# Attention of a fused graph block: three fp16 hi/lo products on 64x64 tiles in place of block-diagonal float32 products

## The chip, the cores and the metric

One core of one Trainium2 chip runs the whole program. The metric is the device time of one execution in microseconds (us), here the median of three runs. The profile is one more execution, taken by the hardware profiler; its times are given from the start of its span.

## The reference

`x` is (128, 64, 512): 128 batches of 64 nodes with 512 features. `adj` is a symmetric 0/1 matrix of 64x64 with ones on its diagonal. Cut to what matters:

```python
# layer 0
x = layernorm(x + (einsum('bnf,nm->bmf', x, adj * adj) + bias))
# layer 1
z_l = einsum('bnd,ed->bne', x, W_lang);  z_g = einsum('bnd,ed->bne', x, W_grav)
v   = einsum('bnd,ed->bne', x, W_V)
zn  = z_l / max(norm(z_l), EPS)
A_l = max(zn @ zn.T, 0) * not_eye                 # 64x64 per batch
d2  = max(|z_g|^2 + |z_g|^2.T - 2 z_g @ z_g.T, 0)
A_g = exp(-d2 / (2 sigma^2)) * not_eye
K_l, K_g = (A * adj) / max(rowsum(A * adj), EPS)  # for A_l and A_g
K   = sigmoid(gate) * K_l + (1 - sigmoid(gate)) * K_g
x   = layernorm(x + (K @ v) @ W_O.T)
```

## The kernel before, in words

The 128 batches are worked on in 16 groups of 8. A group is four pairs of batches: a pair `p` fills the 128 partitions, batch 2p in rows 0 to 63, batch 2p+1 in rows 64 to 127. Each engine has its own instruction stream, written out by hand; semaphores join them. `iteration(g, ...)` is what an engine does for group g, together with the front of group g+1 (`nxt`: layer 0, its normalisation, the split and the transposes) and the end of group g-1 (`before`: attention, residual, final normalisation). Fourteen of the sixteen iterations have both neighbours.

The weights are folded before the loop. Both similarities are quadratic forms, h W'W h', so their matrices are built once (`l_hi`, `l_lo`: the lower triangle with half a diagonal, so that a later step adds the transpose), and W_V and W_O are folded into one matrix (`m_hi`, `m_lo`). Each fp32 factor is split in an fp16 high part and the fp16 rest, and a product is three: hi·hi, hi·lo, lo·hi. fp32 products remain in a few places; a fp32 product shows as two matmuls of the trace.

TensorE does, per iteration (function, line):

- `mix` (L339), four: layer 0 of the next group, fp32, two before and two after `project(g, 0)`.
- `project(g, j)` (L359), j = 0 to 7: 12, 9, 6, 3, 12, 9, 6, 3 products of 512 columns, into three PSUM banks in turn.
- `kernel_t(before)` (L416): transposes the attention matrices `ks_sb` of the group before, behind project 1.
- `attend(before, p)` (L429), four, behind project 2: `kt` is a block-diagonal 128x128 fp32 matrix (two batches, zeros between), `u` is h·M in fp32.
- `values(g, p)` (L375), four of 12 products; `gram` (L389), 96 products of 64 columns, behind values 0; `symmetrise` (L400) behind values 1; `spread` (L409) behind values 2.

ScalarE copies `p_hi` (L557) from PSUM, VectorE subtracts it from PSUM to give `p_lo` (L736); a project's bank is free only then, and gram needs all eight. Likewise `h_hi` on ScalarE (L543) and `h_lo` on VectorE or GpSimd (L731, L1065). ScalarE also copies `u` (L562) and `kt` (L580), applies the final normalisation to `o` (L593), and issues the eight DMA transposes per group (L550), spread between its instructions, which bring h_hi and h_lo to `ht_hi`, `ht_lo`, with features on the partitions. VectorE does the residual o = attention + h (L811), statistics (L713, L815), the normalisation h (L726), and the chain from `t_diag` through `diag`, `nsq`, `vec` to `v_diag` and from `ps_v` to the weights `ks_sb`. GpSimd does the inverse standard deviations (L1026, L1028), two h_lo, `t_diag` (L1048) and inverse norms (L1054, L1055), in this order. SyncE issues the x loads and the stores of a whole group.

The order in which the VectorE stream takes p_low, residual and norm_rows, and the order of p_high and h_high on ScalarE, are fixed by the text of their `iteration`.

Of the kernel before, what the change touches and what calls it, by code (L numbers as in the profile page):

```python
# [28 lines left out]
P = 128  # L29
# [25 lines left out]
def resnorm_graph_kernel(nc, x, adj, bias, w_lang, w_grav, w_v, w_o, gate, log_sigma, out):  # L55
# [18 lines left out]
    with ctx:  # L74
# [16 lines left out]
        ht_lo = [sb(f"ht_lo{i}", [P, DC, ROWS], F16) for i in range(2)]  # L91
        p_hi = sb("p_hi", [P, DC, GB, 2, N], F16)
        p_lo = sb("p_lo", [P, DC, GB, 2, N], F16)
        u = sb("u", [P, PAIRS, D])
# [10 lines left out]
        kt = sb("kt", [P, PAIRS, P])  # L105
# [22 lines left out]
        w_raw["v"] = u  # L128
# [37 lines left out]
        wv_scale = sb("wv_scale", [P, 1])  # L166
# [51 lines left out]
        u_ready = sem("u_ready")  # L218
# [18 lines left out]
        kt_ready = sem("kt_ready")  # L237
# [18 lines left out]
        def over_batches(square_, lo=0, hi=P):  # L256

            return square_[lo:hi, :].unsqueeze(1).to_broadcast([hi - lo, GB, N])

# [6 lines left out]
        def _(sp):  # L266
# [27 lines left out]
            reload(Group(0, 0))  # L294
            with sp.Fori(0, G // 2 - 2) as i:
                reload(Group(i, 1))
                store(Group(i, 0))
                reload(Group(i + 1, 0))
                store(Group(i, 1))
            last = G // 2 - 2  # L300
            reload(Group(last, 1))
            for g in (Group(last, 0), Group(last, 1), Group(last + 1, 0)):
                store(g)

            end = Group(last + 1, 1)
# [19 lines left out]
        def _(pe):  # L325
# [16 lines left out]
            def project(g, j, first):  # L342
# [6 lines left out]
                if j < 3:  # L349
                    if first:  # L350
                        pe.wait_ge(m_copied, j + 1)
                    else:
                        pe.wait_ge(u_ready, g.prev().count(4, j + 2))
                else:
                    pe.wait_ge(plo_ready, g.count(8, j - 2))
                passes = [(k, a, b) for k in range(c, DC)
                          for a, b in ((l_hi, ht_hi), (l_hi, ht_lo), (l_lo, ht_hi))]
                for n, (k, a, b) in enumerate(passes):
                    mm = pe.matmul(proj[j % 3][:, :], a[s][:, blk(k, c), :], b[g.parity][:, k, :],  # L359
                                   start=(n == 0), stop=(n == len(passes) - 1))  # L360
                mm.then_inc(proj_done, 1)

            def values(g, p, first=False):
# [4 lines left out]
                else:  # L368
                    pe.wait_ge(u_ready, g.count(4, 1))
                passes = [(k, a, b) for k in range(DC)  # L370
                          for a, b in ((ht_hi, m_hi), (ht_hi, m_lo), (ht_lo, m_hi))]
                for n, (k, a, b) in enumerate(passes):
                    if first and p == 0 and n % 3 == 0:
                        pe.wait_ge(wt_lo, 2 + k + 1)
                    mm = pe.matmul(proj[j % 3][:, :], a[g.parity][:, k, p * P:(p + 1) * P], b[:, k, :],  # L375
# [3 lines left out]
            def gram(g, first):  # L379
# [7 lines left out]
                for b in range(GB):  # L387
                    for n, (c, a, t) in enumerate(passes):
                        mm = pe.matmul(ps_t[:, b * N:(b + 1) * N],  # L389
                                       a[:, c, b, :, :].rearrange("p s n -> p (s n)"),  # L390
                                       t[g.parity][:, c, b * N:(b + 1) * N],
# [12 lines left out]
            def spread(g, first):  # L404

                pe.wait_ge(v_ready, g.count(1, 1))
                if not first:
                    pe.wait_ge(kt_ready, g.prev().count(2, 2))
# [22 lines left out]
            def last_residual(g, p):  # L431

                if p < 2:
                    pe.wait_ge(sum_ready, g.prev().count(4, (4, 2)[p]))
                elif p == 2:
                    pe.wait_ge(sum_ready, g.prev().count(4, 3))
                pe.matmul(last_ku_bank[p][:, :], ident[:, :], h[g.parity][:, p, :], start=True, stop=False)

            def back(g):
                kernel_t(g)  # L440
                pe.wait_ge(kt_ready, g.count(2, 2))
                pe.wait_ge(u_ready, g.count(4, 4))
                for p in range(PAIRS):
                    pe.matmul(last_ku_bank[p][:, :], kt[:, p, :], u[:, p, :], start=(p == 3), stop=True).then_inc(ku_done, 1)

            def iteration(g, has_prev, has_next):
# [21 lines left out]
                if has_prev:  # L468
                    for p in range(PAIRS):
# [3 lines left out]
                project(g, 7, first)  # L473
# [8 lines left out]
                else:  # L482
                    last_residual(g, 0)
                    last_residual(g, 1)
# [7 lines left out]
                    last_residual(g, 2)  # L492
# [47 lines left out]
        def _(act):  # L540
            def h_high(g, p):
                act.wait_ge(h_ready, g.count(4, p + 1))
                act.activation(h_hi[:, p, :], h[g.parity][:, p, :], ACT.Copy).then_inc(hhi_ready, 1)  # L543

            def transposes(g, first, last):


                for n in range(first, last):
                    p, part, part_t = n // 2, (h_hi, h_lo)[n % 2], (ht_hi, ht_lo)[n % 2]
                    act.dma_start_transpose(part_t[g.parity][:, :, p * P:(p + 1) * P],  # L550
                                            part[:, p, :]).then_inc(ht_loaded[g.parity], 16)
# [8 lines left out]
            def u_copy(g, p):  # L560
                act.wait_ge(proj_done, g.count(12, 9 + p))
                act.activation(u[:, p, :], proj[(8 + p) % 3][:, :], ACT.Copy).then_inc(u_ready, 1)  # L562
# [13 lines left out]
            def kt_copy(g):  # L576
                act.wait_ge(kt_done, g.count(1, 1))
                for q in range(2):
                    half = slice(q * N, (q + 1) * N)
# [541 lines left out]
```

## Time and profile before

| | |
|---|---|
| median of 3 runs | 627.4 us (626.99 to 628.38) |
| span of the profiled execution, first to last instruction | 625.0 us |
| mean granted TensorE clock | 0.998 of full |
| TensorE busy | 614.2 us (98%) |
| VectorE busy | 444.2 us (71%) |
| ScalarE busy | 242.7 us (39%) |
| GpSimd busy | 155.5 us (25%) |
| attention products (L429), share of the chain that ended last | 8% |
| DMA transposes | 128, 13.4% of the 16 DMA engines' span |

The profiled execution has no time of its own beyond the span: the device time of a run also holds what lies before the first and behind the last instruction, and the median of the runs is 2.4 us above the span. Busy time of TensorE is not the same as columns streamed, since matmuls are pipelined and each is shown until its result is out; the chain in order of time shows what each piece really occupies.

### The profile page before, as it was taken

How to read it: one execution, taken by the hardware profiler on the slowest of the kernel's cores; microseconds unless marked ns; L12 is line 12 of the kernel's file. 1: busy time of each engine (PE TensorE's matmuls, PEld its weight loads, DVE VectorE, ACT ScalarE, POOL GpSimd, SP SyncE). 2: the span in 40 equal slices, each digit the busy share in tenths (PEclk: the TensorE clock that was granted, in tenths of full speed). 3: DMA queues.
4: the chain of work that ended last, by engine and by line, in shares of the span. 5: the costliest groups of instructions: out<-in, count | busy, mean ns of one | idle time of the engine just before them, and what ended most of it. 6: DMA issues, size and time to landing. Idle time of an engine off the chain costs nothing.

```text
span 625.0 us, 11961 instructions
## 1 busy us (share of the span) xinstructions
PE 614.2 (98%) x4468; PEld 315.0 (50%) x4468; DVE 444.2 (71%) x940; ACT 242.7 (39%) x413; POOL 155.5 (25%) x159
## 2 busy tenths in 40 slices
PE   9999999999999999999999999999999999999994
PEld 6543545454454545454454545445454545545452
DVE  1759486877868586876868687786858788686564
ACT  2345224333443424434432433344342443443333
POOL 1002205032231403123230503223140312323021
PEclk9999999999999999999999999999999999999999
DMA  8722203434123342423223342312334242302103
GB/s 269 244 44 87 51 1 68 136 53 125 52 62 116 64 134 60 141 42 87 90 50 134 67 134 55 120 51 58 119 67 134 59 143 42 92 17 51 69 2 135
DMA packets 89392, 55.05 MB, mean 88 GB/s; under 512 B 70816, under 2 KB 70816, under 8 KB 89376
## 3 DMA queue, kind: packets, MB, share of 16 engines
q1 hardware_dynamic: 19744, 38.05, 17.9%
q10 hardware_dynamic: 69632, 16.79, 13.4%
q8 instruction: 10, 0.16, 0.1%
q14 instruction: 6, 0.05, 0.0%
HBM read 21.27 MB, written 16.78 MB: 61 GB/s over the span
## 4 chain that ended last, share of the span: by engine, by line
PE 96%; DVE 2%; ACT 1%; POOL 0%; issue 0%; POOLq 0%; ACTq 0%; DVEq 0%
PE proj L359 31%; PE proj L375 27%; PE front L339 9%; PE ps_t L389 7%; PE front L429 4%; PE ps_k L429 4%; PE ps_t L400 3%; PE ps_v L409 2%; PE proj L499 2%; PE proj L529 2%; PE ps_v L416 2%; PE ps_t L499 1%; PE ps_k L329 1%; DVE p_lo L736 1%; PE ps_t L529 1%; DVE y L709 0%
## 5 line engine op out<-in xcount | busy, mean ns | idle before, releaser
L557 ACT ACTIVATE p_hi<-proj 128x512 f16<-128x512 f32 x128 | 75.9, 593 | 118.2 <-PE proj L359 117.7
L736 DVE TENSOR_TENSOR p_lo<-proj,p_hi 128x512 f16<-128x512 f32 x128 | 86.0, 688 | 20.9 <-ACT p_hi L557 17.9
L375 PE MATMUL proj<-m_hi,ht_hi 128*128 128x512 f16 x256 | 97.2, 380 | 0.7 <-DVE p_lo L736 0.7
L375 PE MATMUL proj<-m_hi,ht_lo 128*128 128x512 f16 x256 | 97.0, 379 | 0.0
L375 PE MATMUL proj<-m_lo,ht_hi 128*128 128x512 f16 x256 | 97.0, 379 | 0.0
L1026 POOL TENSOR_TENSOR ve<-mv,eps_ln 128x4 f32<-128x4 f32 x31 | 6.6, 212 | 307.7 <-DVE mv L718 211.5
L562 ACT ACTIVATE u<-proj 128x512 f32<-128x512 f32 x64 | 37.9, 592 | 82.7 <-PE proj L375 82.5
L543 ACT ACTIVATE h_hi<-h 128x512 f16<-128x512 f32 x64 | 36.5, 619 | 69.0 <-DVE h L726 69.0
L1065 POOL TENSOR_TENSOR h_lo<-h,h_hi 128x512 f16<-128x512 f32 x30 | 41.5, 1403 | 84.4 <-ACT h_hi L543 84.4
L359 PE MATMUL proj<-ht_hi,l_grav_hi 128*128 128x512 f16 x160 | 60.6, 379 | 0.6 <-DVE p_lo L736 0.6
L359 PE MATMUL proj<-ht_hi,l_lang_hi 128*128 128x512 f16 x160 | 60.8, 380 | 0.0
L359 PE MATMUL proj<-ht_lo,l_grav_hi 128*128 128x512 f16 x160 | 60.6, 379 | 0.0
L359 PE MATMUL proj<-ht_hi,l_grav_lo 128*128 128x512 f16 x160 | 60.6, 379 | 0.0
L359 PE MATMUL proj<-ht_lo,l_lang_hi 128*128 128x512 f16 x160 | 60.6, 379 | 0.0
L359 PE MATMUL proj<-ht_hi,l_lang_lo 128*128 128x512 f16 x160 | 60.6, 379 | 0.0
L339 PE MATMUL front<-x_in,wmix 128*128 128x512 f32 x128 | 60.2, 593 | 0.0
L593 ACT ACTIVATE o<-o,nmr,rstd 128x512 f32<-128x512 f32 x60 | 46.9, 807 | 9.7 <-issue 9.3
L709 DVE TENSOR_TENSOR y<-front,bias_b 128x512 f32<-128x512 f32 x64 | 42.5, 686 | 11.3 <-PE front L339 10.8
L389 PE MATMUL ps_t<-ht_hi,p_lo 128*128 128x64 f16 x512 | 46.5, 193 | 0.0
L389 PE MATMUL ps_t<-ht_lo,p_hi 128*128 128x64 f16 x512 | 46.5, 193 | 0.0
L389 PE MATMUL ps_t<-ht_hi,p_hi 128*128 128x64 f16 x512 | 46.5, 193 | 0.0
L389 PEld LDWEIGHTS ps_t<-ht_hi,p_hi 128*128 128x128 f16 x512 | 45.1, 98 | 2.3 <-issue 0.5
(166 smaller groups left out, 1051.8 us busy)
## 6 DMA issues: line engine op xcount, KB each, us to landing
x_in<-in_x SPq DMA_DIRECT2D x16, 1024.0 KB, 7.1
out<-o SPq DMA_DIRECT2D x15, 1024.0 KB, 5.0
w_raw_lang<-in_L_gnn_W_lang SPq DMA_DIRECT2D x4, 256.0 KB, 3.1
o<-in_L_gnn_W_O SPq DMA_DIRECT2D x1, 1024.0 KB, 10.2
w_raw_grav<-in_L_gnn_W_grav SPq DMA_DIRECT2D x4, 256.0 KB, 10.1
u<-in_L_gnn_W_V SPq DMA_DIRECT2D x1, 1024.0 KB, 12.0
ht_hi<-h_hi ACTq DMA_TRANSPOSE x64, 2.4
ht_lo<-h_lo ACTq DMA_TRANSPOSE x64, 2.5
```

The lines of the kernel that those rows point to most:

```text
L339: pe.matmul(front[p % 2][:, :], wmix[:, :], x_in[g.parity][:, p, :], start=True, stop=True).then_inc(l0_done, 1)
L359: mm = pe.matmul(proj[j % 3][:, :], a[s][:, blk(k, c), :], b[g.parity][:, k, :], start=(n == 0), stop=(n == len(passes) - 1))
L375: mm = pe.matmul(proj[j % 3][:, :], a[g.parity][:, k, p * P:(p + 1) * P], b[:, k, :], start=(n == 0), stop=(n == len(passes) - 1))
L389: mm = pe.matmul(ps_t[:, b * N:(b + 1) * N], a[:, c, b, :, :].rearrange("p s n -> p (s n)"), t[g.parity][:, c, b * N:(b + 1) * N], start=( ...
L429: pe.matmul(ku_bank[p][:, :], kt[:, p, :], u[:, p, :], start=True, stop=True).then_inc(ku_done, 1)
L543: act.activation(h_hi[:, p, :], h[g.parity][:, p, :], ACT.Copy).then_inc(hhi_ready, 1)
L557: act.activation(p_hi[:, j % 4, :, j // 4, :], by_batch(proj[j % 3]), ACT.Copy).then_inc(phi_ready, 1)
L562: act.activation(u[:, p, :], proj[(8 + p) % 3][:, :], ACT.Copy).then_inc(u_ready, 1)
L593: act.activation(o[:, p, :], o[:, p, :], ACT.Identity, scale=rstd2[:, p:p + 1], bias=nmr2[:, p:p + 1]).then_inc(out_ready, 1)
L709: dve.tensor_tensor(y[:, p, :], front[p % 2][:, :], bias_b[:, :], ALU.add).then_inc(y_ready, 1)
L736: dve.tensor_tensor(p_lo[:, j % 4, :, j // 4, :], by_batch(proj[j % 3]), p_hi[:, j % 4, :, j // 4, :], ALU.subtract).then_inc(plo_ready, 1)
L1065: pool.tensor_tensor(h_lo[:, p, :], h[g.next().parity][:, p, :], h_hi[:, p, :], ALU.subtract).then_inc(hlo_ready_pool, 1)
```

## The change

`u` and `kt` are kept as fp16 pairs (`u_hi`, `u_lo`; `kt_hi`, `kt_lo`, no zero blocks). The attention of a group is two halves `a` = 0, 1; each has three passes (hi·hi, lo·hi, hi·lo as above) of four products with 64 rows, 64 output partitions and 512 columns, on the four quadrants of the array. Half 0 follows project 3, half 1 follows project 4, and the waits stand ahead of the last product of that project. For this the batches of a pair in `ht`, and so in `u`, are paired anew: the transposes take 64 rows and 1024 columns each (two pairs of batches), and are issued by SyncE (only those of the first group still by ScalarE), with `h_hi`, `h_lo` and `ht` laid out by feature chunk. SyncE's loop is written out. VectorE gets `u_low` and `kt_low`; the residual applies a scale; norm_rows is cut in two, and h_low moves behind the p_low. The last group no longer adds h through TensorE (`last_residual`), but by residual. Cut to its core:

```diff
-        h_hi = sb("h_hi", [P, PAIRS, D], F16)
-        h_lo = sb("h_lo", [P, PAIRS, D], F16)
-        ht_hi = [sb(f"ht_hi{i}", [P, DC, ROWS], F16) for i in range(2)]
+        h_hi = sb("h_hi", [P, 2, DC, 2, P], F16)
+        h_lo = sb("h_lo", [P, 2, DC, 2, P], F16)
+        ht_hi = [sb(f"ht_hi{i}", [P, PAIRS, DC, P], F16) for i in range(2)]
...
+        def transposes(queue, g, a):
+            for split, split_t in ((h_hi, ht_hi), (h_lo, ht_lo)):
+                for j in range(2):
+                    queue.dma_start_transpose(
+                        split_t[g.parity][:, 2 * a + j, :, :].rearrange("p c (q n) -> p (c q) n", q=2),
+                        split[j * N:(j + 1) * N, a, :, :, :].rearrange("p c q e -> p (c q e)"),
+                    ).then_inc(ht_loaded[g.parity], 16)
...
+            def turn(g):
+                sp.wait_ge(hlo_ready, g.count(2, 4))
+                transposes(sp, g, 0)
+                sp.wait_ge(hlo_ready_pool, g.count(2, 0))
+                transposes(sp, g, 1)
+            groups = [Group(n // 2, n % 2) for n in range(G)]
+            reload(groups[0])
+            for n, g in enumerate(groups):
+                if n + 3 < G:
+                    reload(groups[n + 1])
+                if n + 1 < G:
+                    turn(groups[n + 1])
+                if n > 0:
+                    store(groups[n - 1])
...
-            def attend(g, p, mixed):
-                if mixed and p in (1, 2):
-                    pe.wait_ge(y_ready, mixed.count(4, p + 2))
-                if p == 0:
-                    pe.wait_ge(kt_ready, g.count(2, 2))
-                    pe.wait_ge(u_ready, g.count(4, 4))
-                elif p == 3:
-                    pe.wait_ge(sum_ready, g.count(4, 1))
-                pe.matmul(ku_bank[p][:, :], kt[:, p, :], u[:, p, :], start=True, stop=True).then_inc(ku_done, 1)
+            def attend_waits(g, a, nxt):
+                if a == 0:
+                    pe.wait_ge(ktlo_ready, g.count(1, 1))
+                    pe.wait_ge(ulo_ready, g.count(4, 4))
+                else:
+                    pe.wait_ge(sum_ready, g.count(4, 1))
+                if nxt:
+                    pe.wait_ge(y_ready, nxt.count(4, 3 + a))
+            def attend(g, a, banks):
+                passes = ((kt_hi, u_hi), (kt_hi, u_lo), (kt_lo, u_hi))
+                for n, (kt, u) in enumerate(passes):
+                    for q in range(2):
+                        half = slice(q * N, (q + 1) * N)
+                        for side in range(2):
+                            mm = pe.matmul(banks[2 * a + q][side * N:(side + 1) * N, :], kt[half, 2 * a + side, :],
+                                           u[half, 2 * a + side, :], start=(n == 0), stop=(n == len(passes) - 1))
+                mm.then_inc(ku_done, 1)
...
                 project(g, 2, first)
-                if has_prev:
-                    for p in range(PAIRS):
-                        attend(before, p, nxt)
-                for j in range(3, 7):
+                for a in range(2):
+                    project(g, 3 + a, first, (before, a, nxt) if has_prev else None)
+                    if has_prev:
+                        attend(before, a, ku_bank)
+                for j in range(5, 8):
                     project(g, j, first)
...
+            def u_low(g, p):
+                dve.wait_ge(uhi_ready, g.count(4, p + 1))
+                dve.tensor_tensor(u_lo[:, p, :], proj[(8 + p) % 3][:, :], u_hi[:, p, :],
+                                  ALU.subtract).then_inc(ulo_ready, 1)
+            def kt_low(g):
+                dve.wait_ge(kthi_ready, g.count(1, 1))
+                dve.tensor_tensor(kt_lo[:, :, :], ps_v[:, 0:PAIRS * N].rearrange("p (a n) -> p a n", a=PAIRS),
+                                  kt_hi[:, :, :], ALU.subtract).then_inc(ktlo_ready, 1)
```

VectorE, the middle of an iteration, from the second p_low to the statistics of the output. Before (o is the residual, h the normalised rows, y and stats layer 0 and its statistics):

```order
L736 TENSOR_TENSOR p_lo<-proj,p_hi 128x8x64
L718 BN_AGGR mv<-stats 128x2 x4
...
L811 TENSOR_TENSOR o<-ps_k,h 128x512
...
L736 TENSOR_TENSOR p_lo<-proj,p_hi 128x8x64
L722 ISA
L726 TENSOR_SCALAR h<-y,mv,rstd 128x512 x4
L731 TENSOR_TENSOR h_lo<-h,h_hi 128x512
L735 REGISTER_ALU
L736 TENSOR_TENSOR p_lo<-proj,p_hi 128x8x64
L731 TENSOR_TENSOR h_lo<-h,h_hi 128x512
```

The same place in the changed stream, from p_low(4) on:

```order
L738 TENSOR_TENSOR p_lo<-proj,p_hi 128x8x64
L823 SCALAR_TENSOR_TENSOR o<-front,ku_scale,h 128x512
L823 SCALAR_TENSOR_TENSOR o<-ps_k,ku_scale,h 128x512
...
L728 TENSOR_SCALAR h<-y,mv,rstd 128x512
...
L738 TENSOR_TENSOR p_lo<-proj,p_hi 128x8x64
L727 REGISTER_ALU
L728 TENSOR_SCALAR h<-y,mv,rstd 128x512 x2
...
L738 TENSOR_TENSOR p_lo<-proj,p_hi 128x8x64
L733 TENSOR_TENSOR h_lo<-h,h_hi 128x4x128 x2
L828 BN_STATS stats<-o 128x6 x4
```

The four h stood behind the third p_lo, ahead of five more; now two stand between the fifth and the sixth, two between the sixth and the seventh, and the h_lo behind the eighth, ahead of the statistics.

ScalarE, the same stretch, before:

```order
L557 ACTIVATE p_hi<-proj 128x8x64
L542 ISA
L543 ACTIVATE h_hi<-h 128x512
...
L543 ACTIVATE h_hi<-h 128x512
L556 REGISTER_ALU
L557 ACTIVATE p_hi<-proj 128x8x64
L542 REGISTER_ALU
L543 ACTIVATE h_hi<-h 128x512
```

And changed, from p_high(4) to p_high(7):

```order
L578 ACTIVATE p_hi<-proj 128x8x64
L571 ISA
L572 ACTIVATE h_hi<-h 128x4x128
L571 REGISTER_ALU
L572 ACTIVATE h_hi<-h 128x4x128
L577 REGISTER_ALU
L578 ACTIVATE p_hi<-proj 128x8x64
L571 REGISTER_ALU
L572 ACTIVATE h_hi<-h 128x4x128
L571 REGISTER_ALU
L572 ACTIVATE h_hi<-h 128x4x128
L577 REGISTER_ALU
```

Three h_hi stood between p_hi 2 and 3 and one between 3 and 4; now two stand between p_hi 4 and 5, two between 5 and 6.

## Rows read from the trace of the kernel before

**Rows 1.** The page: busy time, and the chain that ended last by engine

```profile
PE 614.2 (98%) x4468; PEld 315.0 (50%) x4468; DVE 444.2 (71%) x940; ACT 242.7 (39%) x413; POOL 155.5 (25%) x159
...
PE 96%; DVE 2%; ACT 1%; POOL 0%; issue 0%; POOLq 0%; ACTq 0%; DVEq 0%
```

**Rows 2.** The chain in order of time, 312 to 364 us: start us, us, what

```profile
314.71 2.80 PE ps_t L389 x96
...
321.18 2.69 PE proj L375 x12
...
323.88 0.86 PE ps_v L409 x2
...
327.32 1.72 PE front L339 x4
...
337.31 0.86 PE ps_k L429 x2
...
340.74 7.12 PE proj L359 x33
...
363.07 1.29 PE front L339 x3
```

**Rows 3.** Timeline of VectorE, 327 to 364 us: start, us, engine, line, work [idle before]

```profile
336.10 0.69 DVE L736 TENSOR_TENSOR p_lo<-proj,p_hi 128x512 f16<-128x512 f32 x1
...
347.90 1.31 DVE L736 TENSOR_TENSOR p_lo<-proj,p_hi 128x512 f16<-128x512 f32 x2 [0.63 <-ACT p_hi L557]
349.13 2.46 DVE L815 BATCH_NORM_STATS2 stats<-o 128x6 f32<-128x512 f32 x4
...
351.70 0.37 DVE L821 BATCH_NORM_AGGREGATE mv<-stats 128x2 f32<-128x6 f32 x4
...
355.40 0.69 DVE L742 TENSOR_REDUCE diag<-t_diag 128x8 f32<-128x512 f32 x1 [1.77 <-POOL t_diag L1048]
...
358.13 0.69 DVE L750 TENSOR_TENSOR v_diag<-eye,vec 128x512 f32<-128x512 f32 x1 [1.65 <-POOL vec L1054]
...
360.51 0.69 DVE L762 SCALAR_TENSOR_TENSOR s_sb<-s_sb,ps_v 64x512 f32<-64x512 f32 x1 [1.09 <-PE ps_v L409]
```

**Rows 4.** Timeline of TensorE, first products of symmetrise

```profile
355.77 0.27 PE L400 MATMUL ps_t<-eye_l,t_sb 128*64 128x64 f32 x1
355.78 0.27 PE L400 MATMUL ps_t<-eye_g,t_sb 128*64 128x64 f32 x1
```

**Rows 5.** Groups by line and form: count, busy us, mean ns, idle before

```profile
L375 PE MATMUL proj<-m_hi,ht_hi 128*128 128x512 f16 x256 | 97.2, 380 | 0.7 <-DVE p_lo L736 0.7
...
L736 DVE TENSOR_TENSOR p_lo<-proj,p_hi 128x512 f16<-128x512 f32 x128 | 86.0, 688 | 20.9 <-ACT p_hi L557 17.9
L557 ACT ACTIVATE p_hi<-proj 128x512 f16<-128x512 f32 x128 | 75.9, 593 | 118.2 <-PE proj L359 117.7
...
L726 DVE TENSOR_SCALAR h<-y,mv,rstd 128x512 f32<-128x512 f32 x64 | 30.5, 540 | 2.1 <-POOL rstd L1028 2.1
...
L580 ACT ACTIVATE kt<-ps_v 64x256 f32<-64x256 f32 x32 | 12.1, 378 | 2.0 <-PE ps_v L416 1.2
```

**Rows 6.** Timeline of GpSimd, 352 to 356 us

```profile
352.15 0.20 POOL L1026 TENSOR_TENSOR ve<-mv,eps_ln 128x4 f32<-128x4 f32 x1 [5.09 <-DVE mv L821]
352.43 1.01 POOL L1028 TENSOR_TENSOR rstd<-ve,minus_half 128x4 f32<-128x4 f32 x1
354.10 1.27 POOL L1048 TENSOR_TENSOR t_diag<-t_sb,eye 128x512 f32<-128x512 f32 x1 [0.67 <-ACT t_sb L570]
```

**Rows 7.** Timeline of ScalarE, the h_hi of three pairs

```profile
342.55 1.67 ACT L543 ACTIVATE h_hi<-h 128x512 f16<-128x512 f32 x3 [4.61 <-DVE h L726]
```

**Rows 8.** Timeline of ScalarE's queue, and the page's DMA issues

```profile
347.90 1.20 ACTq L550 DMA_TRANSPOSE ht_hi<-h_hi  x1
349.14 1.29 ACTq L550 DMA_TRANSPOSE ht_lo<-h_lo  x1
...
ht_hi<-h_hi ACTq DMA_TRANSPOSE x64, 2.4
```

More of the change, by code:

```diff
@@ L104, in resnorm_graph_kernel @@
         ks_sb = sb("ks_sb", [P, ROWS])
-        kt = sb("kt", [P, PAIRS, P])
+        kt_hi = sb("kt_hi", [P, PAIRS, N], F16)
+        kt_lo = sb("kt_lo", [P, PAIRS, N], F16)
         stats1 = sb("stats1", [P, PAIRS, 6])
@@ L293, in _ @@
             load(Group(0, 1))
[L294 to L305, printed above, removed]
+            def turn(g):
[12 more added lines that the diff above has]
+                    store(groups[n - 1])
+            end = groups[-1]
             for p in range(PAIRS):
@@ L340, in mix, with project @@
                           start=True, stop=True).then_inc(l0_done, 1)
-            def project(g, j, first):
+            def project(g, j, first, attended=None):
                 c, s = j % 4, ("lang", "grav")[j // 4]
@@ L542, in h_high @@
                 act.wait_ge(h_ready, g.count(4, p + 1))
[L543 to L551, printed above, removed]
+                act.activation(by_chunk(h_hi, p), chunks(h[g.parity], p), ACT.Copy).then_inc(hhi_ready, 1)
             def p_high(g, j, first):
@@ L617, in iteration @@
                 if has_prev:
-                    kt_copy(before)
+                    kt_high(before)
                 p_high(g, 2, first)
+                p_high(g, 3, first)
+                p_high(g, 4, first)
                 if has_next:
@@ L805, in scale_rows, with residual @@
                 dve.tensor_tensor(by_batch(ks_sb), by_batch(a_sb), over_columns(cfac), ALU.mult).then_inc(ks_ready, 1)
-            def residual(g, p, first):
-                dve.wait_ge(ku_done, g.count(4, p + 1))
-                if p == 0 and not first:
+            def residual(g, p, banks):
+                dve.wait_ge(ku_done, g.count(2, p // 2 + 1))
+                if p == 0:
                     dve.wait_ge(o_moved, g.prev().count(16, 32))
-                dve.tensor_tensor(o[:, p, :], ku_bank[p][:, :], h[g.parity][:, p, :], ALU.add).then_inc(sum_ready, 1)
+                dve.scalar_tensor_tensor(out=o[:, p, :], in0=banks[p][:, :], scalar=ku_scale[:, 0:1],
+                                         in1=h[g.parity][:, p, :], op0=ALU.mult, op1=ALU.add).then_inc(sum_ready, 1)
             def out_stats(g, p):
@@ L930, in iteration @@
                 p_low(g, 5)
+                if has_next:
+                    norm_rows(nxt, 1, before)
                 if first:
@@ L934, in iteration @@
                 p_low(g, 7)
+                if has_next:
+                    h_low(nxt, 0)
+                    h_low(nxt, 1)
                 if has_prev:
@@ L944, in iteration @@
                 diagonals(g)
+                u_low(g, 1 if has_next else 0)
                 diagonal_matrices(g)
                 sums(g)
+                if not has_next:
+                    u_low(g, 1)
                 distances(g)
+                u_low(g, 2)
             dve.memset(ones[:, :], 1.0).then_inc(dve_const, 1)
```

177 lines of the change are left out of this document (80 added, 97 removed).

## The prediction

> **What bounds the kernel now.** I read the page first. TensorE is busy for 98% of the span and the chain that ended last runs over it for 96% [rows 1]: as it stands, a microsecond of TensorE removed from a group would be a microsecond gained, if nothing else comes last in its place. Next the chain in order of time. The reader is to see that one group is 35.75 us (the mixes of two groups start at 327.32 and 363.07), that the pieces follow each other without a gap, and that the attention products fill it from 337.31 to 340.74, so 3.43 us [rows 2]. Then VectorE and GpSimd, since the change puts work there: they are off the chain, but not by much. The chain's stamps lie 0.16 us behind the starts of the other views (it follows ends). So gram starts at 314.71 + 35.75 - 0.16 = 350.30, and the last p_lo ends at 347.90 + 1.31 = 349.21: 1.09 us ahead. The spread starts at 323.88 + 35.75 - 0.16 = 359.47, and v_diag ends at 358.82: 0.65 us ahead [rows 2, 3]. These two distances decide the case.
>
> **What TensorE saves.** A full 512-column fp16 product costs 7.12/33 = 0.216 us [rows 2]. The new attention is two halves of twelve 64x64 products each. Whether four such tiles run together no row shows. What rows show is two column tiles running together: an eye_l and an eye_g product start 10 ns apart and run 0.27 us beside each other [rows 4]. The two column tiles there have their own moving data. I take four together, so three rounds, 0.65 us a half. A change of tile shape costs about 0.10 us on each side: the twelve products behind the two-column tiles take 2.69 [rows 2] in place of 12 x 0.216 = 2.59, and I put the same on the way in. A half is then 0.85, both are 1.70, and TensorE saves 3.43 - 1.70 = 1.73 us a group. Ends: two together, 2 x (1.30 + 0.20) = 3.0; one at a time, 24 x 0.216 + 0.4 = 5.6.
>
> The Trainium skill (TensorE: Matmul & The Clock Gate, Part 3, on packing) gives 3.07 times, not 4, for four row tiles; by that, as an estimate, a half is 1.04 and the result some 4 us later. No row here shows row tiles at all.
>
> **What is added elsewhere.** VectorE gets four u_lo (psum in, fp16 out, the form of p_lo, 0.69 each [rows 5]; four instructions of that length in a row take 2.46, so they start 0.60 apart [rows 3]) and kt_lo, half as wide; between ScalarE's kt of the same width, 0.378, and p_lo's 0.69 [rows 5] I take 0.42. The residual keeps its size as a scalar_tensor_tensor. ScalarE has one kt_hi for two kt and loses the issue of transposes. What matters is where the moved steps stand: norm_rows of the next group now comes behind p_low(4) and all four residuals, its second half behind p_low(5); h_high(0), (1) stand ahead of p_high(5), h_high(2), (3) ahead of p_high(6); h_low and the four statistics follow p_low(7). Four waits of TensorE result. I price each from its release, with 0.03 us from one engine's end to the next one's start (t_diag ends at 355.37, diag starts at 355.40 [rows 3, 6]) and 0.16 us from a product's issue slot to its end (0.379 - 0.216 [rows 5]).
>
> *Wait A, ahead of the last product of project 3, for kt_lo.* Now VectorE goes from s_sb at 360.51 (1.04 us behind the spread's start) to the end of the second p_lo at 336.10 + 0.69, one period on: 12.03 us [rows 3]. Two u_lo add 1.2 and kt_lo 0.33 behind p_lo; they fill some 0.4 of small waits of that stretch. So kt_lo is there 1.04 + 13.2 = 14.2 after the spread's start. TensorE's own work to that product is 337.31 - 323.88 = 13.43, plus two products: 13.86 [rows 2]. Stall 0.35.
>
> *Wait B, values(0) for p_lo 5.* From the end of project 4's slots: 0.16 to its end, p_hi 0.60, p_lo, residual, residual at 0.60 each, norm 0.54, two h_hi at 0.53 (three take 1.67 [rows 7]), p_hi 0.60, p_lo 0.69 [rows 5], hand-overs: 5.6 us. TensorE has attend(1) 0.85 and projects 5 to 7, 18 products, 3.89: 4.74. Stall 0.87.
>
> *Wait C, gram for p_lo 7.* From p_lo 5's end: norm, started 0.09 before, ends at 0.45, h_hi at 0.48 and 1.01, p_hi 6 at 1.53, p_hi 7 at 2.02 (a tenth inside the one before, as with h_hi), p_lo 6 at 2.16, p_lo 7 from 2.77 to 3.46. TensorE has values(0), 2.59. Stall 0.87.
>
> *Wait D, spread for v_diag.* From p_lo 7's end: two h_lo end their slots at 1.11, statistics and aggregates take 2.94 (349.13 to 352.07), GpSimd's ve and rstd are done 1.37 later, so at 5.42. t_sb is long there, but t_diag is behind rstd in GpSimd's queue: it ends at 6.72. From t_diag's end (355.37) to v_diag's (358.82) is 3.45 [rows 3, 6]: 10.2. TensorE needs 323.88 - 314.71 = 9.17 from gram to spread [rows 2]. Stall 1.0.
>
> The stalls sum to 3.09, TensorE saves 1.73: **a group grows by 1.36 to 37.1 us**. Fourteen such iterations give 19.0. The first one has no attention to save and C-like waits: 0.7, an estimate. In the last, three products with ident go (2.6) and 1.73 is saved, but gram then stands on p_lo, four u_lo come ahead of the degrees with nothing of TensorE beside them (2.4), and the residuals come between the products and the statistics (1.2, at both halves): with what overlaps I estimate +2.5 net. Sum 22.2: span 625.0 + 22.2 = 647.2. The timed runs' median, 627.4, is 2.4 above the profiled span, so 649.6, **650 us**.
>
> **At nothing:** the transposes. A group has eight; on ScalarE's queue each occupies 1.20 to 1.29 us, the next starts 1.24 behind it, and one lands 2.4 us after its issue [rows 8]. On SyncE the 64-row ones carry the same bytes; I take the same 1.24. The first goes out 1.1 us behind p_lo 7, the last lands at 1.1 + 7 x 1.24 + 2.4 = 12.2, and project 0 of the next group wants it behind the spread (10.2), from where spread, values(3) and two mixes take (327.32 - 323.88) + 1.72 = 5.16: 15.4 [rows 2]. Cover 3.2 us; SyncE waits before and behind it (x load at the mixes, store behind the last normalise) fall outside that stretch. Cover gone, each group pays eight times the excess over 1.6 us apiece. ht's new layout costs TensorE nothing: same columns.
>
> The Trainium skill (TensorEngine Tiling (Array Packing), PSUM Bottleneck) says that tiling speeds up TensorE but not the emptying of PSUM. Here it is the emptying that grows too: five more VectorE reads of PSUM a group.
>
> **The rivals.** *1. The queues keep up, and the saving stays.* Place: the releases of values(0), gram and spread; price -1.73 x 15 = -26, about 601. It decides if the four waits together are under 1.73 in place of 3.09, and gives the full figure at zero. For it: today p_lo keeps 1.09 us ahead and TensorE waited for it 0.7 us in all behind project 7 [rows 3, 5]. Against it: B and C are strings of instructions with known lengths, and each exceeds TensorE's work by almost 0.9. If half the stalls show, the result is near 627. *2. Only two tiles together.* Attention then 3.0 a group, 1.3 more; the 0.65 in the second half mostly fills wait B, so 0.9 more a group: 663. *3. One at a time*, the change not doing what it says: 3.9 more, of which B swallows 0.87: about 692. Against both: column pairs do run together [rows 4]. *4. A 64-row transpose takes twice as long to issue.* The last lands at 1.1 + 7 x 2.4 + 3.6 = 21.5 in place of 15.4 available: 6 us a group, about 740. For it: half the rows, twice the length, no row of it here; against: same bytes.
>
> **How the numbers follow.** Forecast 0.65, its own range 640 to 660 (0.1 us on each of four waits, 0.15 on each half of attention, 14 times: some 10 us each way); half the stalls or fewer, 0.16 (0.13 of it faster, 0.02 within 0.2%, 0.01 slower); two together 0.11; one at a time 0.03; slow transposes 0.05. The range 634 to 666 takes in the forecast, case 2 and the near part of the half-stall case. A measurement of this kernel can tell about 0.2% from no change (runs spread 626.99 to 628.38). Faster 0.13, same 0.02, slower 0.85.
>
> **What would show it.** Right: the new attention lines as starts of four within a few ns, about 0.65 us a half; TensorE busy share down to near 90%; idle ahead of the values line and of gram put down to p_lo, ahead of spread put down to v_diag, near 0.9, 0.9 and 1.0 us a group; GpSimd's t_diag starting where rstd ends. Wrong: idle under 0.4 us a group (rival 1); starts 0.1 or 0.2 us apart in attention (2, 3); TensorE waiting for ht at project 0 (4).

## The result, and the profile after

| | before | after |
|---|---|---|
| median of four runs each | 627.43 us (626.99 to 628.38) | 657.44 us (656.19 to 658.03) |
| span of the profiled execution | 625.0 us | 656.2 us |
| one group, start of its output statistics to the next | 35.75 us | 37.56 us |
| mean granted TensorE clock | 0.998 | 0.989 |

The changed kernel takes 1.0474 times as long, 95% interval 1.0459 to 1.0489: slower by 30.0 us. The forecast was 650 with a range of 634 to 666. The profiled span grew by 31.2 us: fourteen full iterations give 14 x 1.81 = 25.3 of it, and 5.9 lies before and behind them.

The page of the changed kernel, the lines that answer to [rows 1]:

```profile
PE 598.2 (91%) x4718; PEld 293.9 (45%) x4718; DVE 503.0 (77%) x1024; ACT 236.8 (36%) x397; POOL 147.5 (22%) x158
...
DVE 32%; issue 26%; PE 22%; POOL 10%; ACT 8%; ACTq 1%; DVEq 1%; POOLq 0%
```

TensorE has less to do and no longer fills the chain that ended last: its 96% have become 22%. VectorE now has 32% of it, and 26% is "issue", time in which an engine of the chain waited for nothing that the profile shows.

Where TensorE waits, from the view of waits (engine, work, releaser: us in all, times, longest):

```profile
PE proj L405 <- DVE p_lo L738: 11.7, 15, 0.8
PE ps_v L439 <- DVE v_diag L762: 10.3, 14, 0.7
PE ps_t L419 <- issue: 10.1, 14, 0.7
...
PE proj L389 <- DVE kt_lo L748: 6.3, 14, 0.5
```

These are the forecast's waits B, D, C and A, all four, in each of the fourteen groups. Gram's (ps_t) is shown as "issue"; in the kernel gram waits for all eight p_hi and all eight p_lo. What B and C cost can be read from the starts of TensorE's products, here around values(0) and gram:

```profile
323.92 0.38 PE L389 MATMUL proj<-ht_hi,l_grav_lo 128*128 128x512 f16 x1
325.11 0.39 PE L405 MATMUL proj<-m_hi,ht_hi 128*128 128x512 f16 x1 [0.81 <-DVE p_lo L738]
...
327.49 0.38 PE L405 MATMUL proj<-m_hi,ht_lo 128*128 128x512 f16 x1
328.59 0.19 PE L419 MATMUL ps_t<-ht_hi,p_hi 128*128 128x64 f16 x1 [0.72 <-issue]
```

The starts are 1.19 and 1.10 us apart where a product takes 0.216, so B costs 0.97 us and C 0.88.

The attention of one half, timeline of TensorE, with the last product of project 3 ahead and project 4 behind:

```profile
353.24 0.39 PE L389 MATMUL proj<-ht_hi,l_lang_lo 128*128 128x512 f16 x1 [0.45 <-DVE kt_lo L748]
353.56 0.40 PE L467 MATMUL ps_k<-uv,kt_hi 64*64 64x512 f16 x2
353.56 0.40 PE L467 MATMUL front<-uv,kt_hi 64*64 64x512 f16 x2
353.80 0.38 PE L467 MATMUL ps_k<-uv,kt_hi 64*64 64x512 f16 x2
353.80 0.38 PE L467 MATMUL front<-uv,kt_hi 64*64 64x512 f16 x2
354.01 0.38 PE L467 MATMUL ps_k<-uv,kt_lo 64*64 64x512 f16 x2
354.02 0.38 PE L467 MATMUL front<-uv,kt_lo 64*64 64x512 f16 x2
...
354.33 0.39 PE L389 MATMUL proj<-ht_hi,l_grav_hi 128*128 128x512 f16 x1
```

Four tiles start together and the next four 0.21 to 0.24 us later. From 353.24 to 354.33 are 1.09 us; less one full product, 0.216, the half costs 0.87.

### The profile page after: what moved, and what is told of

Read it like the earlier page. It is cut to its first block, busy times and chain, and to the rows that moved or that the text cites. A ratio compares the mean times of both kernels' runs of the same rounds, so it can differ in the third digit from the quotient of the medians.

```text
span 656.2 us, 12404 instructions
## 1 busy us (share of the span) xinstructions
PE 598.2 (91%) x4718; PEld 293.9 (45%) x4718; DVE 503.0 (77%) x1024; ACT 236.8 (36%) x397; POOL 147.5 (22%) x158
## 4 chain that ended last, share of the span: by engine, by line
DVE 32%; issue 26%; PE 22%; POOL 10%; ACT 8%; ACTq 1%; DVEq 1%; POOLq 0%
PE proj L389 9%; DVE y L711 4%; POOL vec L1079 4%; ACT p_hi L578 4%; DVE o L823 3%; DVE stats L715 3%; DVE stats L828 3%; POOL t_diag L1073 3%; DVE p_lo L738 3%; DVE h L728 3%; PE ps_v L439 3%; PE ps_k L467 2%; POOL h_lo L1090 2%; DVE w_sb L779 2%; DVE ks_sb L817 2%
## 5 line engine op out<-in xcount | busy, mean ns | idle before, releaser
L578 ACT ACTIVATE p_hi<-proj 128x512 f16<-128x512 f32 x128 | 74.2, 591 | 159.4 <-PE proj L389 159.3
L405 PE MATMUL proj<-m_hi,ht_hi 128*128 128x512 f16 x256 | 97.4, 380 | 11.7 <-DVE p_lo L738 11.7
L1090 POOL TENSOR_TENSOR h_lo<-h,h_hi 128x512 f16<-128x512 f32 x30 | 34.3, 1165 | 133.0 <-ACT h_hi L572 133.0
L583 ACT ACTIVATE uv<-proj 128x512 f16<-128x512 f32 x64 | 37.9, 592 | 57.8 <-PE proj L405 57.8
L419 PE MATMUL ps_t<-ht_hi,p_hi 128*128 128x64 f16 x512 | 46.4, 193 | 12.3 <-issue 10.1
L743 DVE TENSOR_TENSOR uv<-proj,uv 128x512 f16<-128x512 f32 x64 | 43.8, 684 | 4.7 <-ACT uv L583 2.7
```

The source lines that it names most:

```text
L405: mm = pe.matmul(proj[j % 3][:, :], a[g.parity][:, p, k, :], b[:, k, :], start=(n == 0), stop=(n == len(passes) - 1))
L419: mm = pe.matmul(ps_t[:, b * N:(b + 1) * N], a[:, c, b, :, :].rearrange("p s n -> p (s n)"), t[g.parity][:, b // 2, c, b % 2 * N:(b % 2 + ...
L578: act.activation(p_hi[:, j % 4, :, j // 4, :], by_batch(proj[j % 3]), ACT.Copy).then_inc(phi_ready, 1)
L583: act.activation(u_hi[:, p, :], proj[(8 + p) % 3][:, :], ACT.Copy).then_inc(uhi_ready, 1)
L743: dve.tensor_tensor(u_lo[:, p, :], proj[(8 + p) % 3][:, :], u_hi[:, p, :], ALU.subtract).then_inc(ulo_ready, 1)
L1090: pool.tensor_tensor(by_chunk(h_lo, p), chunks(h[g.next().parity], p), by_chunk(h_hi, p), ALU.subtract).then_inc(hlo_ready_pool, 1)
```

## The experiments

Each was compared with runs of the kernel before on its own chip; those had medians of 627.7 to 627.9 us. A period is the distance of one group's output statistics from the next one's.

**The transposes alone.** The kernel before, its 128-row transposes issued by SyncE in a written-out loop (the first group's still by ScalarE):

```diff
-                    transposes(nxt, 0, 1)
...
+            def turn(g):
+                sp.wait_ge(hlo_ready, g.count(2, 4))
+                transposes(sp, g, 0, 4)
+                sp.wait_ge(hlo_ready_pool, g.count(2, 0))
+                transposes(sp, g, 4, 8)
```

> The kernel before with one part of the change alone: its eight 128-row transposes per group go out on SyncE's queue, behind the h_lo, and ScalarE issues none but the first group's. Order theory (TensorE's new waits come from where normalisation, h_hi and h_lo stand on VectorE, ScalarE and GpSimd): no change, 627 us within 0.3%, since eight issues of 1.24 us end long before project 0 asks for ht. Transpose theory (the move to SyncE costs part of the 30 us): 630 us or more, with TensorE waiting for ht at project 0.

627.53 us, ratio 0.9996 (0.9986 to 1.0005), period 35.75. Moving the transposes to SyncE costs nothing and gives nothing.

**The normalisation alone.** The same kernel, with norm_rows, h_high and h_low where the change puts them, and the attention of before:

```diff
+                    norm_rows(nxt, before, (0, 1))
...
+                    norm_rows(nxt, before, (2, 3))
...
+                    h_low(nxt, 0)
+                    h_low(nxt, 1)
```

> The kernel of e1 (attention products of before, fp32 and block-diagonal, and the residuals in their old place) with only the normalisation moved as in the change: norm_rows in two halves behind p_low(4) and p_low(5), h_high in pairs ahead of p_high(5) and p_high(6), the h_lo behind p_low(7). Order theory: values(0) waits about 0.6 us for p_lo 5, gram 0.9 for p_lo 7, spread 1.0 for v_diag, nothing saved on TensorE, so a group of 38.2 us and 663 us in all, slower than the change itself. Tile theory (what costs is in the new attention: tiles, shape changes, or the extra VectorE work for u_lo and kt_lo): within 1% of 627 us.

661.14 us, ratio 1.0526 (1.0509 to 1.0544), period 38.18. The slowdown is here without a single product of the new attention. Three of the waits of TensorE in this kernel:

```profile
PE proj L388 <- DVE p_lo L726: 5.6, 15, 0.4
PE ps_v L422 <- DVE v_diag L740: 10.4, 14, 0.8
PE ps_t L402 <- issue: 10.1, 14, 0.7
```

The last two are the same as in the changed kernel to 0.1 us. The wait for p_lo ahead of values(0) is half as long (11.7 us there), and there is no kt_lo to wait for.

**ScalarE's order.** The changed kernel, with each p_hi ahead of the h_hi:

```diff
                 p_high(g, 4, first)
+                p_high(g, 5, first)
                 if has_next:
                     h_high(nxt, 0)
                     h_high(nxt, 1)
-                p_high(g, 5, first)
+                p_high(g, 6, first)
+                p_high(g, 7, first)
                 if has_next:
                     h_high(nxt, 2)
                     h_high(nxt, 3)
-                p_high(g, 6, first)
-                p_high(g, 7, first)
```

> The changed kernel with one edit on ScalarE: h_high(0), (1) behind p_high(5) in place of ahead of it, h_high(2), (3) behind p_high(7). VectorE's text is untouched. Order theory: values(0) and gram no longer wait, the wait of spread falls from 0.7 to about 0.25, the one for kt_lo stays at 0.45: a group of 34.7 us, 618 us in all, faster than the kernel before. Tile theory: still above 650 us.

645.57 us, ratio 1.0274 (1.0254 to 1.0294), period 36.74: a miss by 28 us. The waits of values and gram are gone as expected. But the spread's wait grew from 10.3 to 25.0 us. The cause stands in the timelines of VectorE and GpSimd. First the changed kernel:

```profile
363.81 2.27 POOL L1090 TENSOR_TENSOR h_lo<-h,h_hi 128x512 f16<-128x512 f32 x2 [9.05 <-ACT h_hi L572]
...
365.97 1.28 DVE L733 TENSOR_TENSOR h_lo<-h,h_hi 128x512 f16<-128x512 f32 x2
```

Then this experiment:

```profile
320.37 2.72 POOL L1089 TENSOR_TENSOR h_lo<-h,h_hi 128x512 f16<-128x512 f32 x2 [8.40 <-ACT h_hi L572]
320.53 3.12 DVE L732 TENSOR_TENSOR h_lo<-h,h_hi 128x512 f16<-128x512 f32 x2
```

In the changed kernel GpSimd's two h_lo have nearly ended when VectorE's begin. Here both engines begin within 0.16 us, and VectorE's two take 3.12 us in place of 1.28. They lie on the string to v_diag, so this string is 1.84 us longer than the expectation had it; 14 x 1.84 = 25.8 of the 28 us. Seen one by one, the four of this experiment alternate:

```profile
320.37 1.16 POOL L1089 TENSOR_TENSOR h_lo<-h,h_hi 128x512 f16<-128x512 f32 x1 [8.40 <-ACT h_hi L572]
320.53 1.55 DVE L732 TENSOR_TENSOR h_lo<-h,h_hi 128x512 f16<-128x512 f32 x1
321.49 1.61 POOL L1089 TENSOR_TENSOR h_lo<-h,h_hi 128x512 f16<-128x512 f32 x1
322.00 1.64 DVE L732 TENSOR_TENSOR h_lo<-h,h_hi 128x512 f16<-128x512 f32 x1
```

Each but the first starts while the other engine's is running, and ends 0.55, 1.02 and 0.54 us behind that one's end, which is about its own length alone. Whether it is the meeting that slows them was tested twice:

**One engine for h_lo.** The kernel of the last experiment, with all four h_lo on VectorE (SyncE's waits for them follow):

```diff
-                    h_low(nxt, 0)
-                    h_low(nxt, 1)
+                    for p in range(PAIRS):
+                        h_low(nxt, p)
...
-                        pool.tensor_tensor(by_chunk(h_lo, p), chunks(h[g.next().parity], p), by_chunk(h_hi, p),
-                                           ALU.subtract).then_inc(hlo_ready_pool, 1)
```

> e3_norm_behind with all four h_lo on VectorE and none on GpSimd. In e3 VectorE's two h_lo took 3.12 us beside GpSimd's two, against 1.28 in the changed kernel, where the two engines don't overlap. Contention theory: alone, a h_lo is back at about 0.68 us, the four start 0.61 apart and take 2.5, which is 0.6 less than the two beside GpSimd's; the spread's wait falls by as much, 14 times, so 645.6 - 8 = about 637: twice the work on the engine and less time. Rival, that h_lo is slow there for another reason (h_hi just written, the memory): each of the four stays at 1.55, 6.2 in all, the spread's wait grows by 3.1 a group and the time is near 689.

635.80 us, ratio 1.0132 (1.0115 to 1.0149), period 36.09. Its h_lo, from the timeline, and all of them together (ns min/median/max):

```profile
314.74 2.48 DVE L732 TENSOR_TENSOR h_lo<-h,h_hi 128x512 f16<-128x512 f32 x4
```

```profile
L732 DVE TENSOR_TENSOR h_lo<-h,h_hi x64: 680/684/689, 24.5 to 569.2; 128x512 f16<-128x512 f32 x64
```

Four take 2.48 us alone, two took 3.12 beside GpSimd; the period falls by 0.65, and 3.12 - 2.48 is 0.64.

**The old layout.** The kernel of the second experiment (attention and tiles of the kernel before) with the ScalarE order of the third, so that the h_lo meet there too:

```diff
                 p_high(g, 4, first)
+                p_high(g, 5, first)
                 if has_next:
                     h_high(nxt, 0)
                     h_high(nxt, 1)
-                p_high(g, 5, first)
...
                 p_high(g, 7, first)
                 if has_next:
+                    h_high(nxt, 2)
+                    h_high(nxt, 3)
                     u_copy(g, 0)
```

> e2_moved_norm (attention and layout of the kernel before) with ScalarE's h_high as in e3_norm_behind: (0), (1) behind p_high(5), (2), (3) behind p_high(7), so that VectorE's and GpSimd's h_lo meet, on tiles laid out by pair. Contention theory: VectorE's two take about 3.1 us there too, the waits for p_lo go (5.6 us, and 10.1 for gram), the spread's grows by about 1: 655 to 659. Rival, that the layout by feature chunk is what slows them in e3: they stay at 1.28 for two, and the time is 661.1 - 14 x (0.5 + 0.85) = about 642.

657.15 us, ratio 1.0468 (1.0452 to 1.0484), period 37.77.

```profile
326.75 2.72 POOL L1056 TENSOR_TENSOR h_lo<-h,h_hi 128x512 f16<-128x512 f32 x2 [10.71 <-ACT h_hi L556]
326.91 3.11 DVE L720 TENSOR_TENSOR h_lo<-h,h_hi 128x512 f16<-128x512 f32 x2
```

The same 3.11 us on contiguous tiles: the layout is not the cause, the meeting is. The Trainium skill (SBUF — State Buffer, "SBUF: two separate sides") says that a VectorE instruction with two SBUF inputs and a GpSimd instruction that reads SBUF share a pair of ports as an exclusive lock: whichever starts first has it for its whole length. The traces agree: in the third experiment the four h_lo alternate, and with one engine at a time, 1.13 each on GpSimd and 0.60 from start to start on VectorE, they would take 3.5 us; free of each other 2.3; they take 3.27 from the first start to the last end.

**The diagonal first.** The changed kernel, wait D alone taken away:

```diff
-                if has_prev:
-                    ln2(g.prev())
                 if has_next:
                     t_diagonal(g)
+                if has_prev:
+                    ln2(g.prev())
...
                 diagonals(g)
+                if has_prev and has_next:
+                    out_shift(before)
```

> The changed kernel with two steps exchanged: GpSimd makes t_diag ahead of the output's inverse standard deviation, and VectorE makes nmr behind the diagonals. My theory (the four waits are separate, each with its own string) says that only the spread's wait goes: it was 10.3 us over 14 groups beside about 0.1 of restart each, so 657.4 - 11 = about 646, with the waits for kt_lo, p_lo and gram as they were (6.3, 11.7 and 10.1 us). Rival: the waits share one cause, so that taking one only moves its time to the next; then 655 or above. Other rival: they feed each other, so that it falls by more than 15.

644.16 us, ratio 1.0262 (1.0245 to 1.028), period 36.55. The spread's wait is gone, the others stand at 11.7, 10.1 and 6.2 us. Wait D is 1.01 us a group.

**All four.** The third experiment's edit, the diagonal first, and on VectorE the statistics of pairs 2 and 3 behind kt_low, their moments behind p_low(2):

```diff
-                    for p in (2, 3):
-                        row_stats(nxt, p)
-                    dve.wait_ge(stats1_ready, nxt.count(4, 4))
                 p_low(g, 1)
                 if has_prev:
                     kt_low(before)
                 if has_next:
-                    row_moments(nxt)
+                    for p in (2, 3):
+                        row_stats(nxt, p)
+                    dve.wait_ge(stats1_ready, nxt.count(4, 4))
                 if first:
                     m_low(1)
                 p_low(g, 2)
+                if has_next:
+                    row_moments(nxt)
```

> The changed kernel with the edit of e3, and in addition t_diagonal ahead of ln2 on GpSimd with out_shift behind diagonals on VectorE (wait D), and row_stats(2), (3) behind kt_low (wait A). Order theory: all four waits of TensorE gone, a group of 33.9 to 34.1 us (35.75 less 1.73), 605 to 609 us in all. Tile theory: above 650 us. If VectorE as a whole (77% busy in the change) is the bound and not the order, it stays above 615 us with TensorE still waiting.

610.01 us, ratio 0.9716 (0.97 to 0.9732), period 34.07: faster than both kernels. No wait is left that comes in each group, so 34.07 is TensorE's own work, and the saving of 1.73 a group is real: 35.75 - 1.73 = 34.02. VectorE's h_lo still take 1.55 us at the median. In the period they cost nothing any more, but the transposes go out behind them, and twice in the run these now come last. TensorE waits there for ht_lo, 2.3 us in all. The chain of this run has the second of the two:

```profile
541.09 3.04 DVE h_lo L732 x2
...
553.30 3.30 DMA ht_lo<-h_lo
```

**Without the kt_low edit.** The same, less its third part:

```diff
+                    for p in (2, 3):
+                        row_stats(nxt, p)
+                    dve.wait_ge(stats1_ready, nxt.count(4, 4))
                 p_low(g, 1)
                 if has_prev:
                     kt_low(before)
                 if has_next:
-                    for p in (2, 3):
-                        row_stats(nxt, p)
-                    dve.wait_ge(stats1_ready, nxt.count(4, 4))
+                    row_moments(nxt)
                 if first:
                     m_low(1)
                 p_low(g, 2)
-                if has_next:
-                    row_moments(nxt)
```

> e4_all_four without its third part: kt_low and the statistics of pairs 2 and 3 stand as in the changed kernel. My theory: only the wait for kt_lo comes back, 6.2 us over 14 groups in e5 and e6 and about 0.1 of restart each, so 610.0 + 7.6 = about 618. Rival, that in e4 the transposes come last now and then, so that part of it is hidden: 612 to 614.

616.96 us, ratio 0.9822 (0.9807 to 0.9837), period 34.70. Wait A is 0.63 us a group.

**One pass of attention, twice.** In the changed kernel and in the one with all four edits:

```diff
-                passes = ((kt_hi, u_hi), (kt_hi, u_lo), (kt_lo, u_hi))
+                passes = ((kt_hi, u_hi),)
```

> The changed kernel, with only the hi.hi pass of the three in attention: the correction passes kt_hi.u_lo and kt_lo.u_hi are left out (u_lo and kt_lo are still made and waited for). TensorE has 2 x 2 x 0.215 = 0.86 us a group less. My theory: the first half's 0.43 counts, since the string from project 4 to values starts behind it, and the second half's lies inside the wait for p_lo, which grows from 0.8 to 1.2 a group. So 657.4 - 14 x 0.43 - about 1 at the ends = 650. Rival, that TensorE's own work is what the time follows: 657.4 - 13 = 644. Rival, that all is set by the queues: 657.

649.77 us, ratio 1.035 (1.0333 to 1.0367), period 37.13, so 0.43 less; the wait for p_lo grew from 11.7 to 17.8 us. Of the 0.86 us taken from TensorE one half counts, as expected, and the other half is absorbed in wait B.

> The same two passes left out of e4_all_four, whose TensorE never waits in a group. There all 0.86 us a group should count if the four 64x64 tiles of a round stream together (a round 0.215): 610.0 - 14 x 0.86 - about 1 = 597. If the tiles ran two by two (a round 0.43) it would fall by 25 to 585; if the queues behind come last at once (VectorE, the transposes), it stays above 603 with waits for p_lo or ht.

598.01 us, ratio 0.9527 (0.9512 to 0.9543), period 33.38: 0.69 of the 0.86 counts. Two by two, 1.72 would have gone. The missing 0.17 I put down to VectorE, which is busy for 59.25 of 64.74 us there, and for v_diag, whose wait shows 4.1 us over 14 groups at TensorE's weight load; that was not separated.

**The tail.** All four edits, and in the last group u_low(2) behind ks_sb:

```diff
                 distances(g)
-                u_low(g, 2)
+                if has_next:
+                    u_low(g, 2)
...
                 scale_rows(g)
+                u_low(g, 2)
                 u_low(g, 3)
                 kt_low(g)
```

> e4_all_four, and in the last group u_low(2) behind ks_sb, beside kernel_t, where it stood ahead of a_sb. In e4 VectorE ends w_sb at 586.75 and starts a_sb at 588.77, because u_low(2) between them waits for ScalarE's u_hi(2); in the kernel before a_sb follows w_sb by 0.04. So the chain at the end is 2.0 us shorter and 0 to 0.1 comes back at kt_lo: 610.0 - 2.0 = 608. Rival: u_lo(2) and u_lo(3) behind ks_sb delay kt_lo as much; then 610.

608.17 us, ratio 0.9688 (0.9675 to 0.9702). The start of the last attention, first with all four edits, then here:

```profile
592.57 1.12 PE L446 MATMUL ps_v<-eye,ks_sb 128*64 128x64 f32 x16 [3.29 <-DVE ks_sb L816]
...
594.63 0.64 PE L467 MATMUL ps_k<-uv,kt_hi 64*64 64x512 f16 x2 [0.94 <-DVE kt_lo L747]
```

```profile
593.68 0.69 PE L446 MATMUL ps_v<-eye,ks_sb 128*64 128x64 f32 x16 [1.35 <-DVE ks_sb L816]
...
595.31 0.40 PE L467 MATMUL ps_k<-uv,kt_hi 64*64 64x512 f16 x2 [0.94 <-DVE kt_lo L747]
```

TensorE's idle before kernel_t falls from 3.29 to 1.35 us, and behind the shorter idle the products run at full clock: the granted clock is 0.50 from 592.0 to 598.0 in the first trace and 1.00 from 593.5 to 597.5 in the second.

**The best version.** The tail's kernel, with all h_lo on VectorE:

```diff
-                    h_low(nxt, 0)
-                    h_low(nxt, 1)
+                    for p in range(PAIRS):
+                        h_low(nxt, p)
...
-                        pool.tensor_tensor(by_chunk(h_lo, p), chunks(h[g.next().parity], p), by_chunk(h_hi, p),
-                                           ALU.subtract).then_inc(hlo_ready_pool, 1)
```

> e9_tail_u_low with all four h_lo on VectorE, as in e6. In e4 and e9 TensorE waits for ht_lo two or three times in a run (2.3 and 3.1 us): the last of eight transposes lands close to its reader. With the engines apart the first two h_lo are done 1.3 us behind p_lo(7) in place of 3.1, so the transposes start 1.8 us earlier and the waits for ht go: 608.2 - 2 to 3 = 605.5 to 606.5. Rival, that h_lo (2) and (3) load VectorE so that the spread or kt_lo comes late again: 0.1 us or more a group, 610 or above. Rival, that the late transposes have nothing to do with their start: 608.

605.87 us, ratio 0.9652 (0.9639 to 0.9665). Two periods of it, busy time of each engine, then its chain:

```profile
300.00:368.12 68.12, 68.12 (x574) 34.05 (x573) 60.56 (x127) 27.42 (x48) 13.67 (x14) 1.00 0.35 92
```

```profile
PE 92%; DVE 3%; ACT 1%; issue 1%; ACTq 1%; DMA 1%; POOL 0%; POOLq 0%; DVEq 0%
```

TensorE is busy for 68.12 of 68.12 us and is the chain again, and it does not wait for ht_lo any more, for which it waited 3.1 us in the tail's kernel.

## Why the prediction was right, and where it was off

**What TensorE saves: right.** Four tiles run together, 0.87 us a half against 0.85. Rivals 2 and 3 (two or one at a time) are excluded by the starts and by the one-pass runs. The Trainium skill (TensorE: Matmul & The Clock Gate, Part 3) has 3.07 for four row tiles, by which a half was 1.04; that doesn't describe this form, which took 0.87.

**The transposes: right for the changed kernel.** At the median one takes 1.27 us of SyncE's queue in either shape, and TensorE of the changed kernel waits for no ht. Rival 4 is excluded. The cover of 3.2 us held for this order only. With the waits gone, and VectorE's h_lo held up ahead of them, the transposes came last now and then: TensorE waits for ht_lo, 0.5 to 3.1 us in all, in each of the five kernels with the new attention that have the third experiment's order and two h_lo on GpSimd, and for 1.1 us in the one with the diagonal first; in the two with all h_lo on VectorE it does not.

**The four waits.** They make 37.56 - 34.07 = 3.49 us a group; the forecast had 3.09. With a saving of 1.68 in place of 1.73 a group grew by 1.81 where 1.36 was forecast; fourteen times the difference is 6.3 us, most of the 7.4 by which 650 was too low.

| wait | forecast | measured | by |
|---|---|---|---|
| A, kt_lo | 0.35 | 0.63 | with all four edits against without kt_low's |
| B and C, p_lo | 0.87 + 0.87 | 1.85 | the remainder; by the starts 0.97 + 0.88 |
| D, v_diag | 1.0 | 1.01 | the diagonal first |

*A* was the worst sized. From the spread's start to the end of kt_lo I had 14.2 us; the trace of after has it from 338.65 to 352.69 + 0.41 = 353.10, so 14.45, which is most of the 0.28 that A came out longer. Each wait also costs more than its row: the rows have 0.45, 0.78, 0.72 and 0.74, in sum 2.69 a group, and without the waits a group is 3.49 shorter. That is 0.2 for each. 0.16 of it is the time from a product's issue slot to its end, which the sum had; some 0.04 is left, for which it had no term, and which no run takes apart. *B* has a term of the wrong size, too. The residual "keeps its size", I wrote, but as a scalar_tensor_tensor it lasts longer:

```profile
358.37 0.74 DVE L823 SCALAR_TENSOR_TENSOR o<-front,ku_scale,h 128x512 f32<-128x512 f32 x1
359.03 0.74 DVE L823 SCALAR_TENSOR_TENSOR o<-ps_k,ku_scale,h 128x512 f32<-128x512 f32 x1
```

The starts are 0.66 apart, not 0.60, twice on the string: 0.12, against the 0.10 by which B came out longer. *C* was right. *D* was right in its length (from the end of p_lo 7 to that of v_diag 328.49 to 338.60, so 10.1 us against 10.2) and in its step, t_diag behind rstd (1.37 and 1.27 were the terms):

```profile
332.91 1.01 POOL L1053 TENSOR_TENSOR rstd<-ve,minus_half 128x4 f32<-128x4 f32 x1
333.88 1.27 POOL L1073 TENSOR_TENSOR t_diag<-t_sb,eye 128x512 f32<-128x512 f32 x1
333.95 1.23 DVE L838 SCALAR_TENSOR_TENSOR nmr<-mv,rstd 128x4 f32<-128x4 f32 x1 [0.82 <-POOL rstd L1053]
```

**Before and behind the fourteen iterations.** Forecast 3.2 us, measured 5.9. The starts of TensorE's work in the two traces divide the span's growth (us; the mixes stand in each iteration ahead of project 0, the spread follows wait D):

| stretch | before | after | more |
|---|---|---|---|
| start to the first mixes, ahead of the loop | 13.56 | 14.70 | 1.1 |
| to the mixes of iteration 0 | 29.27 | 30.62 | 1.4 |
| to the spread of iteration 0 | 30.68 | 30.51 | -0.2 |
| to the spread of iteration 14 | 500.40 | 525.79 | 25.4 |
| to the end | 51.1 | 54.6 | 3.5 |

The first stretch lies between 13.55 and 14.81 in all fourteen traces, of either layout: its 1.1 us are not the change's. The second is 29.27 in the four traces with the old attention and 30.61 to 30.63 in the ten with the new: the forecast had no term for it. ScalarE's queue issues four transposes of the first group, not three, ahead of the sum of squares of W_grav (L691), at 1.3 us each, and TensorE waits for it:

```profile
34.69 0.38 PE L564 MATMUL ps_k<-ssq,ones 128*128 128x2 f32 x2 [1.28 <-ACT p_lo L691]
```

These two stretches are the 2.5 us beyond the forecast. The first iteration itself, with 0.7 in the forecast, has -0.2; the last, with 2.5, has 3.5. That the two together are what was forecast, 3.3 against 3.2, is luck. In the last iteration two things were missing. u_low(2) stands ahead of a_sb and waits for ScalarE: moving it was worth 1.8 us (610.01 to 608.17). And the last attention ran at half the clock. Windows of the changed kernel (busy of PE, PEld, VectorE, ScalarE, GpSimd; granted clock; share and GB/s of the DMA engines):

```profile
635.00:640.00 5.00, 3.25 (x16) 1.26 (x13) 3.46 (x7) 3.31 (x5) 0.00 (x0) 1.00 0.08 31
640.00:645.00 5.00, 2.51 (x32) 1.59 (x36) 2.38 (x7) 0.38 (x1) 0.00 (x0) 0.65 0.48 179
645.00:650.00 5.00, 1.38 (x16) 0.25 (x8) 4.81 (x12) 0.50 (x1) 0.89 (x2) 0.50 0.00 0
```

TensorE had been idle for 3.3 us ahead of kernel_t, and the clock fell from 2.4 to 1.2 GHz; its rounds there start 0.42 us apart.

**Rival 1, that the saving stays,** failed in the changed kernel and came true with other orders: 605.87 at best, near its 601. In the groups it was a matter of order and not of VectorE's load: in two periods with all four edits that engine is busy for 61.66 of 68.14 us, in the changed kernel for 60.82 of 75.12.

The miss in the experiments, the third one's 618, had one false step: I took h_lo at 0.64 wherever it stood, and did not ask what GpSimd does at that moment.

## What to carry to other kernels

When work is taken from the bounding engine, list for each place where it waits the string of instructions on the other engines that leads there, with their queues' order, and compare its length with what is left on the engine; where the waits that a reordering brings add up to more than the saving, the change is a loss. Price a reordering apart from the arithmetic that it comes with: here the arithmetic was worth -1.7 us a group and the order +3.5. After a reorder look again at which instructions of VectorE and GpSimd now run at the same time, at what is issued behind them, at the stretch ahead of the loop, and at the clock wherever TensorE stands still.

## What the hardware showed unexpectedly

- The h_lo of VectorE and of GpSimd, whose inputs all lie in SBUF, hold each other up: on VectorE one takes 0.68 us alone and 1.55 where they meet, on GpSimd 1.16 and 1.38 (medians). The smallest suffers most: nmr, 128x4, takes 1.23 us beside t_diag and ends with it, and 0.16 where t_diag runs elsewhere. p_lo, which reads PSUM for one of its inputs, keeps its 0.69 throughout; in the kernel before two of them beside GpSimd's h_lo take 1.30.
- Where the kernel before lets them meet for a moment, GpSimd pays and VectorE hardly does: VectorE's h_lo starts at 345.34, 0.17 us ahead of the end of GpSimd's first (344.30 to 345.51), and takes 0.71; GpSimd's second starts inside it, at 345.46, and takes 1.60. That fits a lock that goes to whoever starts first; no run changed this order alone.
- Behind 3.3 us of idle time TensorE ran 16 small products (1.12 us) and its last attention at 1.2 GHz; behind 1.35 us of idle time it ran the same at 2.4 (0.69 us for the small ones). No run looks at what lies between.
